# A weight-staging loop with split transfers, and the place of one gate activation, in an attention-plus-mixture kernel on eight cores

## The reference, cut to what matters

```python
v = zeros; integrated = xf
for _ in range(2):
    ctx = concat([integrated, v])
    shared_ctrl = gelu(ctx @ shared_w1 + shared_b1) @ shared_w2 + shared_b2
    ctrl = experts(ctx)          # gelu(ctx @ w1[e] + b1[e]) @ w2[e] + b2[e], the two chosen experts
    # each ctrl splits into a, b, g:
    #   v_next = sigmoid(a)*v - softplus(b)*(x-mu);  x_next = x + 0.1*sigmoid(g)*v_next
    x_next, v_next = mix of shared and expert results
    halt = sigmoid(gelu(integrated @ halt_w1 + halt_b1) @ halt_w2 + halt_b2)
    integrated = integrated + halt * (x_next - integrated)
    v = v + halt * (v_next - v)
refined = gelu(integrated @ refine_w1 + refine_b1) @ refine_w2 + refine_b2
out = xf + integration_weight * refined
```

## Time and profile before

| what | us |
|---|---|
| median of 2 runs (5916.61 and 5920.03) | 5918.32 |
| the profiled execution | 5926.67 |
| its span on the slowest core, core 3 | 5925.1 |
| spans of all cores | 5876.3 to 5925.1 |

### The profile page before, as it was taken

One profiled execution on the slowest core, in us unless ns is written; L12 is line 12 of the kernel. 1 busy time (PEld: TensorE's weight loads), 2 busy tenths in 40 slices (PEclk: granted clock), 3 DMA queues, 4 the chain that ended last, 5 costly groups with the idle time before them and its releaser, 6 DMA issues.

```text
span 5925.1 us, 46637 instructions; the slowest of 8 cores (5876.3 to 5925.1 us)
## 1 busy us (share of the span) xinstructions
PE 3351.4 (57%) x13546; PEld 1286.9 (22%) x13546; DVE 1957.7 (33%) x3033; ACT 1994.3 (34%) x2251; POOL 1.2 (0%) x7
## 2 busy tenths in 40 slices
PE   1003555444358888555565555588885556555655
PEld 1001111111112222222222222222222222222222
DVE  3135333200222222344443444222223443434443
ACT  0012111100047777223223323377774223323322
POOL 0000000000000000000000000000000000000000
PEclk9999666667678989566666666799997766666666
DMA  5432000154321101112222121201101222121221
GB/s 145 136 94 64 22 22 22 22 18 22 45 65 34 32 20 27 47 61 86 85 68 71 61 82 61 80 26 34 35 18 31 86 68 71 61 82 62 84 86 64
DMA packets 251242, 340.68 MB, mean 57 GB/s; under 512 B 112133, under 2 KB 148997, under 8 KB 247338
## 3 DMA queue, kind: packets, MB, share of 16 engines
q1 hardware_dynamic: 250996, 337.70, 21.4%
HBM read 286.96 MB, written 48.37 MB: 57 GB/s over the span
## 4 chain that ended last, share of the span: by engine, by line
PE 39%; DVE 23%; ACT 15%; DMA 11%; issue 7%; DVEq 2%; ACTq 2%; SPq 1%
ACT af L817 8%; PE pf L464 6%; PE pf L1139 5%; DMA s_v<-af 5%; PE pf L825 4%; PE pf L1431 3%; PE pf L827 3%; PE pf L807 3%; PE pf L810 2%; DMA af<-fw 2%; PE pf L1212 2%; ACTq L1566 1%; PE pf L1141 1%; DVEq L1566 1%; SPq L237 1%
## 5 line engine op out<-in xcount | busy, mean ns | idle before, releaser
L817 ACT ACTIVATE af<-pf 128x1024 bf16<-128x1024 f32 x1024 | 1011.8, 1022 | 460.4 <-PE pf L810 453.8
L464 PE MATMUL pf<-af 128*128 128x512 bf16 (+3 forms) x2784 | 601.7, 391 | 480.4 <-DVE af L630 223.2
L825 PE MATMUL pf<-af 128*65 128x512 bf16 x1024 | 415.2, 405 | 221.6 <-ACT af L817 158.9
L1139 PE MATMUL pf<-af 128*128 128x512 bf16 x1280 | 498.1, 533 | 0.0
L464 PEld LDWEIGHTS pf<-af 128*128 128x128 bf16 (+1 forms) x2784 | 294.6, 129 | 790.9 <-issue 703.7
L807 PE MATMUL pf<-af 65*128 65x512 bf16 x1024 | 418.1, 408 | 84.1 <-DMA af<-af 84.1
L827 PE MATMUL pf<-af 128*65 128x512 bf16 x1024 | 416.1, 406 | 0.0
L810 PE MATMUL pf<-af 65*128 65x512 bf16 x1024 | 415.1, 405 | 0.0
L422 PE MATMUL pb<-af 128*128 128x128 bf16 x256 | 32.4, 306 | 406.0 <-DVE af L416 406.0
L825 PEld LDWEIGHTS pf<-af 128*65 128x65 bf16 x1024 | 114.1, 111 | 640.3 <-issue 632.7
L1473 PE MATMUL pf<-af 128*128 128x512 bf16 x512 | 145.2, 438 | 122.2 <-DMA af<-s_fw 121.7
(11 more groups left out here) (243 smaller groups left out, 4016.7 us busy)
## 6 DMA issues: line engine op xcount, KB each, us to landing
af<-s_fw SPq DMA_DIRECT2D x512, 256.0 KB
af<-s_ew SPq DMA_DIRECT2D x256, 128.0 KB
af<-xb SPq DMA_DIRECT2D x48, 512.0 KB
af<-s_v SPq DMA_DIRECT2D x32, 520.0 KB
af<-fw SPq DMA_DIRECT2D x32, 512.0 KB
af<-s_kt SPq DMA_DIRECT2D x32, 512.0 KB
af<-qkv_w SPq DMA_DIRECT2D x24, 512.0 KB
s_v<-af SPq DMA_DIRECT2D x128, 65.0 KB
```

The source lines that it names most:

```text
L464: last = t.matmul(psum_ap, lhs_list[k], rhs_list[k], start=(start and k == 0), stop=(stop_last and k == n - 1))
L817: tex[kt] = b.op("scalar", lambda sc, kt=kt, sb=sb: sc.activation(out=Abuf[kt & 1], in_=pf[:, sb * 1024:(sb + 1) * 1024], func=AF.Exp, sca ...
L825: t.matmul(pf[0:65, 2048:2560], Vbv[:, kt, :], Abuf[kt & 1][:, 0:512], start=(kt == 0), stop=(kt == 31)),
L1139: t.matmul(ps, hmv[:, hc, :], ew2Rv[:, hc, col:col + 512], start=(hc == 0), stop=False)
```

## The change

There are two edits, which have nothing to do with each other.

The first is in `cast_spill`. The one load of a tile becomes four, of 32 partitions each, and the one spill becomes two, of 64 partitions each. The cast waits for all four loads. Behind the two spills SP gets a no-operation that waits for both of them and raises a semaphore; this is what the load two tiles later, and the later readers of the scratch tensor, wait for.

The second is in `ffn_iter`. `thl` and `thd` move from behind `mmh` to behind the four Gelus `th`, which are taken out of the mask loop and put in a loop of their own ahead of it. The mask loop is otherwise the same: `mmm0` still waits for `thl`.

```diff
-            dl = dma(stf, src_sl, deps=([stg_free[i]] if stg_free[i] else []))
+            prev = [stg_free[i]] if stg_free[i] else []
+            dls = [dma(stf[q * 32:(q + 1) * 32, :], src_sl[q * 32:(q + 1) * 32, :],
+                       deps=prev) for q in range(4)]
             stbf = ab_stg[i][:, 0:cols]
-            ctk = cast(stbf, stf, deps=[dl])
-            sp = dma(dst_dram[rt], stbf, deps=[ctk])
-            stg_free[i] = sp
-            toks.append(sp)
+            ctk = cast(stbf, stf, deps=dls)
+            sp = [dma(dst_dram[rt][0:64], stbf[0:64, :], deps=[ctk]),
+                  dma(dst_dram[rt][64:128], stbf[64:128, :], deps=[ctk])]
+            spn = b.op("sync", lambda e: e.nop(), deps=sp, dma=True)
+            stg_free[i] = spn
+            toks.append(spn)
@@ ffn_iter
-        thl = sop(lambda sc_: sc_.activation(out=X["hlt"], in_=pf[:, 2568:2569],
-                                             func=AF.Sigmoid), deps=[mmh], inc=True)
-        thd = vop(lambda v: v.tensor_scalar(X["hD"], X["hlt"], 0.1, None, ALU.mult),
-                  deps=[thl], inc=True)
@@
-        mask_deps = [C["teqT"]]
-        hm_toks = []
         ex_toks = []
         for hc in range(4):
-            ps = pf[:, hc * 512:hc * 512 + 128]
-            th = sop(lambda sc_, ps=ps, hc=hc: sc_.activation(
-                out=hallTv[:, hc, :], in_=ps, func=AF.Gelu,
-                bias=eb1_pp[:, hc:hc + 1]), deps=[mm_last], inc=True)
+            th = sop(lambda sc_, hc=hc: sc_.activation(
+                out=hallTv[:, hc, :], in_=pf[:, hc * 512:hc * 512 + 128],
+                func=AF.Gelu, bias=eb1_pp[:, hc:hc + 1]), deps=[mm_last], inc=True)
+            ex_toks.append(th)
+        thl = sop(lambda sc_: sc_.activation(out=X["hlt"], in_=pf[:, 2568:2569],
+                                             func=AF.Sigmoid), deps=[mmh], inc=True)
+        thd = vop(lambda v: v.tensor_scalar(X["hD"], X["hlt"], 0.1, None, ALU.mult),
+                  deps=[thl], inc=True)
+        hm_toks = []
+        for hc in range(4):
+            th = ex_toks[hc]
             mmm0 = top(lambda t, hc=hc: t.matmul(
                 pf[:, 2560:2688], sselb[:, hc * 128:(hc + 1) * 128], eq["T0"],
                 start=True, stop=True),
```

More of the change, by code:

```diff
@@ L1262, in ffn_iter @@
             hm_toks += [thm0, thm1]
-            ex_toks += [th]
         A, B = 0, 1024
```

## The result

The changed kernel takes 6146.39 us (median of 11 runs, 6117.33 to 6200.03) against 5917.56 us. The ratio is 1.0376, with a 95% interval from 1.0346 to 1.0406, about 222 us more. (The two medians are 229 us apart; the ratio leaves out the runs in which one half of the chip was slower.) The direction was forecast. The size was not: 158 us were expected, and the time lies 16 us above the range. The spans of the profiled executions are 5925.1 and 6146.1 us, on different cores (3 and 0).

The account below looks back on a forecast made before the run. No engine was taken as near full; staging and blocks were chains priced by the wait that ends last. Blocks 96 plus staging 62 made 158 us more, 5918 + 158 = 6076 us, range 6015 to 6130.

Parts of the forecast that it names:

- What bounds each stage: Whole kernel: no engine near full; staging a serial load, cast, spill loop, blocks a chain priced by the wait ending last.
- Removing 64 set changes costs and gains nothing: Blocks: the 64 removed ACT set changes of 1.283 us lie in longer ACT pauses, so their removal counts as nothing.
- The masks' delay, 96 us: Blocks: `mmm0` waits for the later `thl`, so the mask loop starts 2.62 and 3.35 us later; 96 us over 16 blocks.
- The spill: Staging: SP waits until both spill halves land, 1.87 us more a tile for fw and about 1.6 for ew.
- The load: Staging: with the way free, four part loads take 0.75 us less a tile for fw; nothing gained for ew.
- The one whose quarters land one by one: Rival, staging: the stagger of the four part loads is paid in full; 6171 us, chance 0.06.
- The one with a cheap no-operation: Rival, staging: the no-operation costs next to nothing and loads gain, staging -24 and blocks +96; 5990 us, chance 0.10.
- The one with half of the delay absorbed: Rival, blocks: the masks' delay is half absorbed by the control Sigmoid, 55 us left; 6035 us, chance 0.10.
- that of the other side: Rival, blocks: ACT's set changes were on the path, so the second edit gives -82 us; 5898 us, chance 0.04.
- The upper end: Range's top, 6130 us: 96 for blocks, 85 for loads no quicker, 31 of 45 for a dearer spill.
- the 157 us: Staging's bound from above: 85 us with loads no quicker, plus the part loads' whole stagger on top.
- two signs of being wrong: Blocks and staging: wrong if a block is not some 6 us longer, or the staging ends before 390 us.

Follow-up runs that it names:

- p2_column_thd_late: Kernel before plus the second edit, with the gate's output in its own PSUM column, no mask matmul waiting for `thl`, and `thd` behind the mask loop; ratio 1.0057.
- p2_own_column: Kernel before plus the second edit, with the gate's output in its own PSUM column so no mask matmul waits for `thl`; ratio 1.0173.
- nop_only: Kernel before with whole loads and whole spills, plus only the no-operation that waits for the spill; ratio 1.0133, staging 314.8 us.
- p1_interleaved: Kernel before plus the first edit, with part loads of every fourth partition and part spills of every second; ratio 1.0335, staging 399.4 us.
- loads_in_four: Kernel before plus the no-operation and four part loads, with one whole spill; one run, staging 347.5 us.

## Why the prediction was right or wrong

*What bounds each stage* was right. Both stretches were serial chains, and the 231 us that they grew by came out as 222 in the kernel.

*Removing 64 set changes costs and gains nothing*: right; p2_column_thd_late shows it. The change followed the rule of the Trainium skill that the prediction names, to batch activations by set, and it paid nothing here, since PE was the later one each time. The 1283 ns agree with the trace; the drain of about 1380 ns beside them (page "ScalarE: Activation LUTs", section "What ACT_TABLE_LOAD costs") does not, since the gap ahead of a set change was 0.12 us behind an idle ACT and 0.07 us right behind four Gelus.

*The masks' delay, 96 us*: right in size, 2.53 and 3.26 us measured in the changed kernel against 2.62 and 3.35, and 96.6 us over the blocks. But its reason was only half of it. The prediction put `thd` at nothing, because it ran beside `mmm0`. That is so only while `mmm0` waits as well. In DVE's queue it is a second wait of the same length, and it alone costs the whole delay (p2_own_column, blocks +94 us). Here the forecast had luck: a right sum hid a wrong step, and only the experiment that took the first wait away brought it out.

*The spill*: this term was mis-sized, 1.87 us more a tile for fw and 1.6 for ew, measured 2.57 and 2.23. The wait for a whole spill was well read (2.25 in nop_only, where the same sum gives 2.4). What was wrong was that two halves would land as early as one whole, 2.35. They add 0.8 to 0.85 us. Windows of the two part spills of one tile after, the first of them issued at 122.21:

```profile
123.20:124.05 0.85, 0.00 (x0) 0.00 (x0) 0.00 (x0) 0.00 (x0) 0.00 (x0) 1.00 0.77 178
124.05:124.90 0.85, 0.00 (x0) 0.00 (x0) 0.00 (x0) 0.00 (x0) 0.00 (x0) 1.00 0.57 130
...
122.21:123.00 0.79, 0.00 (x0) 0.00 (x0) 0.00 (x0) 0.00 (x0) 0.00 (x0) 1.00 0.00 0
```

The bytes start about 1.0 us after the issue, not 0.77, and take 1.7 us together at 178 and 130 GB/s, where the whole spill took 1.0 at 262. The prediction had the second half issued 0.48 us behind the first with an issue of 0.33; SP took 0.56 and 0.54. p1_interleaved shows that the slower rows make 0.18 of the 0.8. The estimate by the Trainium skill, page "DMA: Bandwidth & Descriptors", section "Anatomy of one DMA", whose fixed cost is fitted for transfers that GpSimd issues, while SP issued these, was about 0.5 us more a tile. It pointed the right way (0.7 and 0.6 measured), but not by a later receipt: the next load's issue follows the last byte by 0.54 us after and 0.57 in nop_only.

*The load*: the term that failed most. I gave it -0.75 us for fw and nothing for ew. Measured over the cores in the changed kernel it was +0.06 and +0.79. Three steps went wrong.

- The 1.64 us ahead of the first byte were read off one tile, whose load took 5.75 us (124.56 less 118.81) where the mean was 4.46, and taken as a wait behind the spill's bytes that would go down to 0.77. Over all cores and tiles of the kernel before, the first byte of an fw load comes 1.09 us after its issue; in nop_only, where the way is free, 1.01. So 0.08 us was to be won ahead of the first byte, not 0.87; the bytes themselves came 0.2 us quicker, which makes the 0.3 of nop_only. The tile that comes two behind the one of the earlier trace rows has its load issued at 131.20 and its bytes from about 132.2:

```profile
130.72 0.33 SPq L237 DMA_DIRECT2D s_fw<-af  x1
131.20 0.33 SPq L237 DMA_DIRECT2D af<-fw  x1
135.71 0.69 DVE L241 CAST af<-af 128x1024 bf16<-128x1024 f32 x1 [5.12 <-DMA af<-fw]
```

- The 4.46 us are themselves of core 3, whose fw loads were the slowest of the eight. The mean is 4.19, and 0.27 of the promised 0.75 was there already.
- The pieces were taken to land as early as a whole. loads_in_four shows +0.4 and +0.9. The fw bytes did come as early (3.46 us in both), but the cast started 0.4 us later behind them. For ew the same 1.64 left 1.14 us for the bytes of a whole load, where they took 1.6, and in four pieces 2.7. In the changed kernel the ew loads of cores 4 and 5 took 4.6 us and those of the other six 3.8, so 0.2 of the 0.79 is theirs.

Together the load is 32 x 0.8 + 16 x 0.8, 38 us, and the spill 32 x 0.7 + 16 x 0.6, 32 us: 70 of the 73 us that the sum lacked in the staging.

*The rivals.* The one whose quarters land one by one came nearest (6171 us), though not the whole stagger was paid. The one with a cheap no-operation is out; alone it costs 72 us. The one with half of the delay absorbed, and that of the other side, are out by p2_column_thd_late. The upper end had a price for a dearer spill and one for loads no quicker, each near what came; what it lacked was the ew loads getting slower; a range that took in the 157 us that the prediction itself gave as the staging's upper bound would have held the time. Neither of the two signs of being wrong came: a block was 6 us longer, and the staging ended at 484 us. Both looked only for a change that costs less.

## What to carry to other kernels

A transfer cut into pieces on one queue is complete later than a whole one (0.4 to 0.9 us here), and that can pay only where something starts on the first pieces; here nothing could, since one cast waited for all four. Before a wait is read off one tile of a timeline, compare that tile with the mean over tiles and cores. What a serial staging loop needs is the next load issued ahead of the instruction that waits. When an instruction is moved past a slow one, follow its result into every queue that reads it, and look at what stands behind each reader, also where the reader itself is worthless to the path.

## What the runs showed of the hardware

- Rows of 2 KB from 64 adjacent partitions take 138 ns each in a spill, from all 128 or from every second one 86 and 85 ns. It made 0.18 us of the 0.8 by which two halves are later than a whole.
- From the start of an issue on SP to the first byte 0.80 us passed for a whole spill, 1.08 for one in two halves, and 0.95 to 1.1 for a load.
- SP took about 0.32 to 0.42 us to issue a part load of 32 adjacent partitions of fw and 0.50 to 0.59 for one of every fourth (2.41 us for four against 1.71). A whole spill took 0.33, and the two halves 0.45 and 0.54.
- With loads four deep, one core moved 279 GB/s in a stage where all eight did the same; one load at a time gave 136.
